# Loading a 268 MB matrix in rows of 63 KB into two slots instead of rows of 32 KB into four

## What is computed

```python
def reference(x, adj, u):                      # x, u: 8192 x 64, adj: 8192 x 8192, all float32
    keep = (u >= 0.1).astype(x.dtype)
    x_drop = x * keep / (1.0 - 0.1)
    y = x + jnp.matmul(adj, x_drop)
    m = jnp.mean(y, axis=-1, keepdims=True)
    v = jnp.var(y, axis=-1, keepdims=True)
    return (y - m) / jnp.sqrt(v + 1e-05)
```

## Time and profile before

| | |
|---|---|
| median of 3 runs | 648.08 us (648.06 to 648.10) |
| the profiled execution's own time | 648.88 us |
| its span, first to last instruction | 647.0 us |
| PE busy | 507.6 us, 78% of the span |
| DMA | 272.63 MB read, 425 GB/s over the span |
| mean granted TensorE clock | 0.945 of full speed |

### The profile page before, as it was taken

How to read it: one execution, slowest core, us unless ns; L and a number is a source line. 1 busy time by engine, 2 the same in 40 slices (tenths; PEclk the granted TensorE clock), 3 DMA queues, 4 the chain that set the end, 5 groups by cost and what they waited for, 6 DMA issues and landing times.

```text
span 647.0 us, 5290 instructions
## 1 busy us (share of the span) xinstructions
PE 507.6 (78%) x2306; PEld 172.8 (27%) x2306; DVE 48.2 (7%) x227; ACT 10.8 (2%) x18; POOL 17.8 (3%) x27
## 2 busy tenths in 40 slices
PE   0578877987887967878778787878779878688797
PEld 0122222222232322223222232322223223122245
DVE  3100101010010100101000010100101001010001
ACT  0000000000000000000000000000000000000000
POOL 0000000000000000000000000000000000000000
PEclk9988999989988998899988899889988889898899
DMA  9999999999999999999999999999999999999995
GB/s 371 436 426 436 432 427 430 431 446 421 430 430 435 438 427 432 426 439 434 427 430 432 442 425 427 438 430 438 427 432 431 428 438 427 432 438 435 418 421 229
DMA packets 11958, 274.80 MB, mean 425 GB/s; under 512 B 1457, under 2 KB 1713, under 8 KB 3121
## 3 DMA queue, kind: packets, MB, share of 16 engines
q1 hardware_dynamic: 10944, 272.90, 98.2%
q10 hardware_dynamic: 1008, 1.84, 0.7%
HBM read 272.63 MB, written 2.10 MB: 425 GB/s over the span
## 4 chain that ended last, share of the span: by engine, by line
DMA 76%; PE 22%; issue 1%; SPq 0%; another core or an unknown queue 0%; DVE 0%; POOL 0%; POOLq 0%; DVEq 0%
DMA raw<-adj_dram 73%; PE acc L152 21%; DMA raw<-adj_next_dram 3%; PE final_acc L152 0%; SPq L120 0%; SPq L124 0%; POOL rstd L276 0%; PE turned L160 0%; POOLq L46 0%; DVE stats L228 0%; SPq L118 0%; SPq L117 0%; DVE rows L224 0%; DVE final_normed L256 0%
## 5 line engine op out<-in xcount | busy, mean ns | idle before, releaser
L152 PE MATMUL acc<-raw,dropped 128*64 128x512 f32 (+1 forms) x2048 | 482.6, 627 | 107.0 <-DMA raw<-adj_dram 106.6
L152 PEld LDWEIGHTS acc<-raw,dropped 128*64 128x64 f32 x2048 | 149.8, 145 | 427.4 <-issue 278.1
L224 DVE TENSOR_TENSOR rows<-turned,x_sb 128x256 f32<-128x256 f32 (+1 forms) x16 | 6.7, 421 | 562.3 <-PE turned L160 562.3
L276 POOL TENSOR_TENSOR rstd<-var_eps,minus_half 128x4 f32<-128x4 f32 (+1 forms) x16 | 16.0, 1000 | 621.4 <-DVE var_eps L235 621.4
L160 PE MATMUL turned<-join,sums 128*128 128x64 f32 x126 | 17.5, 281 | 10.3 <-ACT sums L197 10.3
L160 PEld LDWEIGHTS turned<-join,sums 128*128 128x128 f32 x126 | 15.3, 191 | 23.7 <-ACT sums L197 23.5
L197 ACT COPY sums<-acc 128x512 f32<-128x512 f32 (+1 forms) x16 | 9.3, 580 | 623.7 <-PE acc L152 623.7
L241 DVE TENSOR_SCALAR normed<-rows,moments,rstd 128x64 f32<-128x64 f32 x63 | 15.5, 310 | 17.9 <-POOL rstd L276 17.9
L168 PE MATMUL final_turned<-x_sb,eye 128*128 128x64 f32 x2 | 0.7, 447 | 18.1 <-DVE dropped L217 18.1
L228 DVE BATCH_NORM_STATS2 stats<-rows 128x6 f32<-128x64 f32 x63 | 9.6, 214 | 0.6
L152 PE MATMUL final_acc<-raw,dropped 128*64 128x128 f32 x128 | 7.4, 274 | 0.0
(11 more groups left out here) (14 smaller groups left out, 2.6 us busy)
## 6 DMA issues: line engine op xcount, KB each, us to landing
raw<-adj_dram SPq DMA_DIRECT2D x60, 4096.0 KB, 31.5
raw<-adj_next_dram SPq DMA_DIRECT2D x1, 3840.0 KB, 31.1
raw<-adj_next_dram SPq DMA_DIRECT2D x1, 3072.0 KB, 27.4
raw<-adj_next_dram SPq DMA_DIRECT2D x1, 2304.0 KB, 24.5
dropped<-u_dram SPq DMA_DIRECT2D x1, 2048.0 KB, 7.9
x_sb<-x_dram SPq DMA_DIRECT2D x1, 2048.0 KB, 12.3
raw<-adj_final_dram SPq DMA_DIRECT2D x2, 1024.0 KB, 15.6
raw<-adj_next_dram SPq DMA_DIRECT2D x1, 1920.0 KB, 17.6
```

Source lines behind the costliest of these rows:

```text
L152: last = nc.tensor.matmul(sum_bank[t * D:(t + 1) * D, 0:width], dropped[:, t * PAIRS + q, :], raw[:, s, start:start + width], start=(q == ...
L224: nc.vector.tensor_tensor(rows[:, 0:groups, :], turned[:, 0:groups, :], x_sb[:, b * GROUPS:b * GROUPS + groups, :], ALU.add).then_inc(rows ...
L276: nc.gpsimd.tensor_tensor(rstd[:, 0:groups], var_eps[:, 0:groups], minus_half[:, 0:groups], ALU.pow).then_inc(rstd_ready, 1)
```

## The change

The 8192 output rows are split as 16 x 504 + 128 instead of 15 x 512 + 384 + 128. Row r of the first 8064 now sits on partition r // 64 of 126, so the blocks' DVE and POOL work and their stores have 126 partitions. There are two slots of 16 pairs; a slot's load is 128 rows of 63 KB (16 x 2 x 504 x 4 bytes), 8064 KB. `raw` has 126 KB per partition. The last 128 rows are loaded as before. Of the x that they need, a load of 128 rows of 256 bytes is added.

The second slot of the last but one block and both slots of the last one are loaded in parts (3 for a first slot, 5 for a second). PE's loop has one body for all blocks, so it waits eight times per block on one semaphore, `landed`, which POOL raises: for each load POOL waits and then adds one, or the number of parts of that slot. The work of DVE, ACT and POOL is looped over blocks or pairs of blocks. PE turns the last 504 rows before it starts on the final 128.

```diff
+ROWS = 126
+GROUPS = 4
+WIDTH = GROUPS * ROWS
+BLOCKS = CHUNKS // GROUPS
+PAIR = TILES * WIDTH
+SLOT_PAIRS = [(0, 16), (16, 32)]
+SLOTS = len(SLOT_PAIRS)
+SLOT = max(q1 - q0 for q0, q1 in SLOT_PAIRS) * PAIR
+PARTS = [(0, 0, 6), (0, 6, 11), (0, 11, 16), (1, 16, 22), (1, 22, 26), (1, 26, 29), (1, 29, 31), (1, 31, 32)]
+IN_SLOT = [sum(part[0] == s for part in PARTS) for s in range(SLOTS)]
...
         @block.sync
...
+            sp.dma_start(x_final[:, :], x[ROWS * CHUNKS:N, :]).then_inc(x_final_loaded, DMA)
             for s in range(SLOTS):
-                sp.dma_start(raw[:, s, :], adj[s]).then_inc(raw_loaded[s], DMA)
-            with sp.Fori(1, BLOCKS) as b:
+                load_slot(0, s)
+            with sp.Fori(1, BLOCKS - 2) as b:
                 for s in range(SLOTS):
                     sp.wait_ge(multiplied, (b - 1) * SLOTS + s + 1)
-                    sp.dma_start(raw[:, s, :], adj[b * SLOTS + s]).then_inc(raw_loaded[s], DMA)
-            pair = TILES * NEXT_WIDTH
-            for n, (s, q_slot, q0, q1) in enumerate(NEXT):
-                sp.wait_ge(multiplied, (BLOCKS - 1) * SLOTS + s + 1)
-                sp.dma_start(raw[:, s, (q0 - q_slot) * pair:(q1 - q_slot) * pair],
-                             adj_next[:, q0 * pair:q1 * pair]).then_inc(next_loaded[n], DMA)
-            sp.wait_ge(multiplied, BLOCKS * SLOTS + 1)
+                    load_slot(b, s)
+            for s in range(SLOTS - 1):
+                sp.wait_ge(multiplied, (BLOCKS - 3) * SLOTS + s + 1)
+                load_slot(BLOCKS - 2, s)
+            sp.wait_ge(multiplied, (BLOCKS - 2) * SLOTS)
+            for n, (s, q0, q1) in enumerate(PARTS):
+                if s == SLOTS - 1:
+                    load_part(BLOCKS - 2, n)
+            for n, (s, q0, q1) in enumerate(PARTS):
+                if q0 == SLOT_PAIRS[s][0]:
+                    sp.wait_ge(multiplied, (BLOCKS - 2) * SLOTS + s + 1)
+                load_part(BLOCKS - 1, n)
+            sp.wait_ge(multiplied, (BLOCKS - 1) * SLOTS + 1)
...
         @block.tensor
...
             with pe.Fori(0, BLOCKS) as b:
-                for s in range(SLOTS):
-                    pe.wait_ge(raw_loaded[s], (b + 1) * DMA)
-                    first = s * PER_PIECE
-                    multiply(acc, WIDTH, s, first, first, first + PER_PIECE).then_inc(multiplied, 1)
+                for n, (s, q0, q1) in enumerate(PARTS):
+                    pe.wait_ge(landed, b * len(PARTS) + n + 1)
+                    last = multiply(acc, WIDTH, s, SLOT_PAIRS[s][0], q0, q1)
+                    if q1 == SLOT_PAIRS[s][1]:
+                        last.then_inc(multiplied, 1)
                 pe.wait_ge(sums_ready, b + 1)
-                turn(GROUPS)
-            for n, (s, q_slot, q0, q1) in enumerate(NEXT):
-                pe.wait_ge(next_loaded[n], DMA)
-                multiply(acc, NEXT_WIDTH, s, q_slot, q0, q1).then_inc(multiplied, 1)
+                for i in range(GROUPS):
+                    last = nc.tensor.matmul(turned[0:ROWS, i, :], sums[:, i * ROWS:(i + 1) * ROWS], join[:, :],
+                                            start=True, stop=True)
+                last.then_inc(block_turned, 1)
             for n, (q0, q1) in enumerate(FINAL):
-                if n == 1:
-                    pe.wait_ge(sums_ready, BLOCKS + 1)
-                    turn(NEXT_GROUPS)
                 pe.wait_ge(final_loaded[n], DMA)
                 last = multiply(final_acc, P, 0, 0, q0, q1)
...
         @block.scalar
...
+            with act.Fori(0, STORES - 1) as r:
+                for k in range(STORED):
+                    take_sums(r * STORED + k)
+                act.wait_ge(normed_ready, r * STORED + STORED)
+                act.dma_start(out_dram[:, bass.ds(r * (STORE_GROUPS * D), STORE_GROUPS * D)],
+                              normed[:, :, :]).then_inc(out_stored, DMA)
...
         @block.vector
...
+            with dve.Fori(0, STORES) as r:
+                for k in range(STORED):
+                    b = r * STORED + k
...
         @block.gpsimd
...
+            def pass_slot(b, s):
+                pool.wait_ge(raw_loaded[s], b * DMA + DMA)
+                pool.sem_inc(landed, IN_SLOT[s])
+            def pass_part(n, loads):
+                pool.wait_ge(part_loaded[n], loads * DMA)
+                pool.sem_inc(landed, 1)
...
+            pass_slot(0, 0)
+            with pool.Fori(0, BLOCKS - 2) as b:
+                for s in range(1, SLOTS):
+                    pass_slot(b, s)
+                pass_slot(b + 1, 0)
+                rsqrt(b)
+            for s in range(1, SLOTS - 1):
+                pass_slot(BLOCKS - 2, s)
+            for n, (s, q0, q1) in enumerate(PARTS):
+                if s == SLOTS - 1:
+                    pass_part(n, 1)
+            for n, (s, q0, q1) in enumerate(PARTS):
+                pass_part(n, 2 if s == SLOTS - 1 else 1)
+                if n == 1:
+                    rsqrt(BLOCKS - 2)
+            rsqrt(BLOCKS - 1)
```

More of the change, by code:

```diff
@@ L1 @@
 from contextlib import ExitStack
-from concourse import mybir
+from concourse import bass, mybir
 P = 128
@@ L32, with dropout_matmul_layernorm @@
 STORE_GROUPS = STORED * GROUPS
+STORES = BLOCKS // STORED
 P_DROP = 0.1
 EPS = 1e-5
-def dropout_matmul_layernorm(nc, x, u, adj, adj_next, adj_final, out):
+def dropout_matmul_layernorm(nc, x, u, adj, adj_final, out):
     fp32 = mybir.dt.float32
@@ L106, in dropout_matmul_layernorm, with load_part, load_slot @@
         out_stored = semaphore("out_stored")
-        next_stored = semaphore("next_stored")
+        last_stored = semaphore("last_stored")
         final_stored = semaphore("final_stored")
         block = ctx.enter_context(nc.Block())
-        def out_groups(first, n):
-            return out_dram[:, first * D:(first + n) * D]
         @block.sync
         def _(sp):
+            def load_part(b, n):
+                s, q0, q1 = PARTS[n]
+                q_slot = SLOT_PAIRS[s][0]
+                sp.dma_start(raw[:, s, (q0 - q_slot) * PAIR:(q1 - q_slot) * PAIR],
+                             adj[b, :, q0 * PAIR:q1 * PAIR]).then_inc(part_loaded[n], DMA)
+            def load_slot(b, s):
+                q0, q1 = SLOT_PAIRS[s]
+                sp.dma_start(raw[:, s, 0:(q1 - q0) * PAIR],
+                             adj[b, :, q0 * PAIR:q1 * PAIR]).then_inc(raw_loaded[s], DMA)
@@ L191, in _, with take_sums @@
         def _(act):
[L192 to L205, removed]
+            def take_sums(b):
+                act.wait_ge(multiplied, b * SLOTS + SLOTS)
+                act.wait_ge(turned_free, b + 1)
+                nc.scalar.copy(sums[:, :], acc[:, 0:WIDTH]).then_inc(sums_ready, 1)
+            act.sem_inc(turned_free, 1)
+            act.sem_inc(out_stored, DMA)
+            with act.Fori(0, STORES - 1) as r:
[4 more added lines that the diff above has]
+                              normed[:, :, :]).then_inc(out_stored, DMA)
+            for b in range(BLOCKS - STORED, BLOCKS):
+                take_sums(b)
             act.wait_ge(final_multiplied, 1)
             nc.scalar.copy(final_sums[:, :], final_acc[:, 0:P]).then_inc(final_sums_ready, 1)
-            act.wait_ge(out_stored, BLOCKS // STORED * DMA)
+            act.wait_ge(out_stored, STORES * DMA)
         @block.vector
@@ L218, in _ @@
                                     ALU.mult).then_inc(x_dropped, 1)
[L220 to L243, removed]
@@ L245, in _ @@
-            for b in range(BLOCKS):
-                normalise(b, GROUPS)
-            normalise(BLOCKS, NEXT_GROUPS)
+            with dve.Fori(0, STORES) as r:
+                for k in range(STORED):
+                    b = r * STORED + k
+                    dve.wait_ge(block_turned, b + 1)
+                    nc.vector.tensor_tensor(rows[:, :, :], turned[0:ROWS, 0:GROUPS, :],
+                                            x_sb[0:ROWS, bass.ds(b * GROUPS, GROUPS), :],
+                                            ALU.add).then_inc(turned_free, 1)
+                    dve.wait_ge(turned_free, b + 2)
+                    for i in range(GROUPS):
+                        last = nc.vector.bn_stats(stats[:, i, :], rows[:, i, :])
+                    last.then_inc(stats_ready, 1)
+                    dve.wait_ge(stats_ready, b + 1)
+                    dve.nop(nofuse=True)
+                    for i in range(GROUPS):
+                        last = nc.vector.bn_aggr(moments[:, i, :], stats[:, i, :])
+                    last.then_inc(moments_ready, 1)
+                    dve.wait_ge(moments_ready, b + 1)
+                    nc.vector.tensor_scalar(var_eps[:, :], moments[:, :, 1], EPS, None,
+                                            ALU.add).then_inc(var_ready, 1)
+                    dve.wait_ge(rstd_ready, b + 1)
+                    if k == 0:
+                        dve.wait_ge(out_stored, (r + 1) * DMA)
+                    for i in range(GROUPS):
+                        last = nc.vector.tensor_scalar(normed[:, k * GROUPS + i, :], rows[:, i, :],
```

(8 more changed lines are left out.)

93 lines of the change are left out of this document (39 added, 54 removed).

## The result

The changed kernel takes **663.31 us** (median, 660.9 to 666.7), the kernel before in the same session 648.09 us. The ratio is 1.0237 with a 95% interval of 1.0213 to 1.0261: slower by 2.4%, where 0.33% faster was forecast, and outside the stated range. The profiled execution took 660.9 us with a span of 659.1, against a forecast span of 644.9.

What follows compares the result with a forecast made beforehand. The DMA engines, above all the slowest, were taken to bound the kernel. Packets -2.0, x_final +0.1, stores +0.6, code -0.9 and tail +0.1 gave -2.1 us: 648.08 to 646.0 us, range 643.9 to 647.0.

Steps and rivals of the forecast that it cites:

- Depth of the queue: Refills with two slots: relay, PE's slot, issue and start fit in the 19.1 us period, so 0 us lost.
- the way from issue to flowing data: Start of a refill's DMA: 1.5 us from the small last store, 3.1 us from the first load on idle engines.
- rival A: Queue runs dry between PE's end of a slot and the other's landing: 0.2 us per refill, +5.8, 651.8 us; chance 0.17.
- copy and turn: After every second slot, 1.7 us of PE's time, leaving it free at 17.7 us, before the landing at 19.1.
- sign of a wrong rate: Forecast is wrong if DMA share stays at 99% and landings are still further apart than 19.15 us.
- the tail: Last blocks' parts and final rows: PE ends 10.8 us after block 15's landing, 10.7 before; +0.1 us, between 0 and +1.7.
- a row of 63 KB is one packet: Loads: 198 fewer packets per engine at 10 ns, -2.0 us, between 0 and -2.4.
- The stores use 14 engines: Stores of 126 partitions: by the skill's divisor rule they use 14 engines, +0.6 us.
- The q14 fetch: Instruction fetch of an unrolled program beside a store: nothing to fetch with loops, -0.9 us, between 0 and -2.1.
- POOL's relay: POOL passing a landing on to PE: 0.16 us by SP's nearest row, at most 0.3 with PE's own wait.
- B: Packets saved, but the engine ending last is late from the fetch, shallow queue or PE's tail: about 647.1 us; chance 0.17.
- C: Loads: rows of 63 KB go as several packets, 232 per engine come back, 2.3 us: 648.3 us; chance 0.08.

## Why the prediction was wrong

**The step that failed** is "Depth of the queue", and in it one term: the way from issue to flowing data, and the 0 for 29 refills that followed from it. I put it between 1.5 us (a 32 KB store of 8 small rows per engine, end to end) and 3.1 us (the first load, on idle engines), took 1.5 by adding it to the slow clock and 3.1 only beside the fast one, and concluded that a refill 2.9 us ahead of the landing would be in time.

Measured, the term is larger. In the 15 refills issued under 4 us ahead, the time from issue to landing less the 19.05 us that the rows take is 3.1 to 5.5 us, 4.6 in the median, stores included. A refill that is 3 to 4 us ahead makes the next landing late by 0.9 us, one under 3 us by 1.4, stores included; from about 4 us on the lateness is 0.1 us or none. The term isn't a late start: where engines were already waiting, the first rows of a refill begin about 1.0 us after its issue. They are slow, 3.3 us instead of 2.38 in the windows above. I also had one landing for all 16 engines, while in the trace they end their part of a slot 0.9 to 2.9 us apart, so that the first has run out of rows well before the landing that I measured the lead from.

A single time from issue to landing doesn't tell the term, since it contains the rest of the other slot. The shortest of 29, 22.1 us, was 3.1 us ahead and lost nothing; the one issued at 187.27, 3.4 us ahead, took 24.6 (view of source line 131, changed kernel):

```profile
DMA to landing us min/median/max: 22.1/23.7/48.7
```

The row nearest to an 8 MB load on the same queue was the 2 MB load, not the small store. With 3.1 us throughout, the slow clock already gave 19.3 us against a period of 19.1, and A would have been the forecast, though at 0.2 us a refill.

**The leads themselves were right in the mean.** PE's slot was forecast at 14.0 to 15.7 us and the lead at 2.9 to 4.6; the slots took 13.74 us in 4 of 30 cases, about 15.4 in most and 16.0 to 16.6 in nine, and the lead was 3.9 in the mean, the single ones 2.1 to 6.3. The Trainium skill (TensorE: Matmul & The Clock Gate, section on oscillation) says that waits for data between tiles can send every tile off at the lower clock. The trace agrees here with 26 of 30. Some lost 2.7 us to it, where I had allowed 1.7 outside rival A. The copy and turn that I put at 1.7 us took 3.1 to 3.9 in every second block, 1.3 of it ACT's table load, so that PE was not always free before the landing, as I had it: in four of these seven blocks it began on the next slot at the end of the turn, up to 0.6 us after the landing.

**Rival A was the outcome**, with its place and its condition, but priced at 0.2 us for each of 29 refills where it costs 0.53 for each of 27, and with 0.17 where the trace held enough for more. Its sign in the profile was half wrong too: landings over 19.2 us apart, yes, but no gaps in the DMA row. Some 10 of the 14.5 us go into longer packets, and the mean of the moved bytes, 417 instead of 425 GB/s, is where to look. The prediction's own sign of a wrong rate came up too, a DMA share near 99% with landings over 19.15 us apart, though a covered load takes the forecast 19.05 us.

**The other terms** hold when the queue is covered, and the run with four pairs left out shows their sum: 646.47 us against 646.0, span 644.6 against 644.9. It shortens the last two blocks' multiplying as well, so the work in its tail isn't the changed kernel's, though the tail is as long. One by one: a row of 63 KB is one packet of 2.38 us, where 2 x 63/64 of the 1.21 us of a row of 32 KB (the earlier trace rows less the semaphore writes) would be 2.39; the packets on q1 are the forecast 7772. The stores use 14 engines: 980 = 7 x (126 + 14) packets. This agrees with the Trainium skill, DMA: Bandwidth & Descriptors, section on why a DMA increments its semaphore by 16. The q14 fetch is gone and the one on q8 stayed. The 0.9 us for the q14 fetch was a little high: in the kernel before, two landings beside a store come 0.61 us later in all for six of the seven stores and 1.35 for the one with that fetch, which leaves 0.74. Another q14 fetch at 184.9 us, beside another store, cost nothing. POOL's relay is 0.09 us from landing to PE, where 0.16 to 0.3 was allowed. In the tail PE ended its last final row 10.7 us after block 15's last landing, forecast 10.8, and the end came 4.4 us later (timeline, 625 to 660 us):

```profile
631.94 13.74 PE L175 MATMUL acc<-raw,dropped 128*64 128x504 f32 x64 [1.90 <-POOLq L290]
...
647.38 7.28 PE L175 MATMUL final_acc<-raw,dropped 128*64 128x128 f32 x128
```

**B and C** play no part: no fetch moved, no row was cut.

## What to carry to other kernels

The buffer's size doesn't say how deep the queue is: count the time from the issue of a refill to the landing of what is still queued, and want more than 4 us of it for loads like these, at the slowest clock that the consumer may meet. Three slots of 11 pairs give 14 us and two of 16 give 4, out of the same SBUF, while the longer row saves 9 ns. For the start of a transfer take the row of a transfer of the same kind and size, and distrust a DMA row full of nines when the mean of the moved bytes falls.

## What was not expected of the hardware

- The lead that a refill needs, about 4 us. Below it the loss isn't a step: refills 3 to 4 us ahead lost from nothing to 1.6 us. Rows at the change took 3.0 us on average instead of 2.38 and counted as busy. Why engines that still had a row of the old slot to move also began the new one slowly stays open, and so does what sets the loss of a single refill; the runs show the price, not the reason.
- The looped ACT code loads its activation table in each of the seven rounds, once per two blocks, and the turn then starts 2.04 us after the last matmul instead of 0.69 to 0.75. With two slots PE then reaches some landings up to 0.6 us late; what that costs no run tells apart, and with the same table loads three slots and four pairs left out lose nothing (the page's groups: count, busy us, mean ns, idle before):

```profile
L212 ACT ACT_TABLE_LOAD x7 | 9.0, 1283 | 300.5 <-PE acc L175 300.5
```

- The changed kernel varies by 6 us from run to run (660.9 to 666.7), the kernel before by 0.1. A likely reason, not tested: with the queue covered a late slot leaves no trace, with a lead near the limit every slow start of a slot does.
